# A small GpSimd fill behind each neighbour gather of a graph kernel's first two layers

## What is computed

```python
# layers 0 and 1, "untyped"
xn = layernorm(h); q, k, v = xn @ wq, xn @ wk, xn @ wv
scores = einsum('ehd,ehd->eh', q[dst], k[src]) * scale      # edges, and one self edge per node
attn = softmax of scores over the edges of each dst
agg = segment_sum(attn * v[src], dst)
h = h + agg @ wo + bo
h = h + gelu(layernorm(h) @ w1 + b1) @ w2 + b2
# layer 2, "typed"
mod_k = K[src] + 0.2 * rel_w[edge_type]
scores = einsum('ehd,ehd->eh', Q[dst], mod_k) / D ** 0.5
msgs = segment_sum(softmax(scores) * V[src], dst)            # V itself where a node has no edge
x = x + layernorm(msgs @ Wo + bo + node_features) * gamma + beta
```

## Time and profile before

| | |
|---|---|
| time before, median of 3 runs | 6028.8 us (6025.58 to 6051.66) |
| the profiled execution | 6041.55 us, of which the span is 6039.4 us |
| busy share of the span: DVE, PE, POOL, ACT | 58%, 54%, 46%, 31% |
| gathers of neighbours' rows (L1283) | 2430, mean 997 ns each |
| share of the 16 DMA engines, all queues | q0 (from POOL) 40.3%, q1 (from SP) 9.4% |
| moved | 886.73 MB, 147 GB/s over the span |
| granted TensorE clock, mean | 0.742 |

### The profile page before, as it was taken

The page is one execution under the profiler, slowest core; times in us unless marked ns, Lnnn a source line. Parts: engine busy times, 40 slices in busy tenths (PEclk is TensorE's granted clock), DMA queues, the critical chain, the costliest instruction groups (busy, mean ns, idle before and its releaser), DMA issues. The chain is left out here.

```text
span 6039.4 us, 88354 instructions
## 1 busy us (share of the span) xinstructions
PE 3256.9 (54%) x17373; PEld 2423.7 (40%) x17374; DVE 3499.7 (58%) x5216; ACT 1879.4 (31%) x4257; POOL 2782.5 (46%) x2783
## 2 busy tenths in 40 slices
PE   8575455455555555635545454455565545555655
PEld 6232334333333344523433343333344434444444
DVE  6441445545555555544555555555554758798887
ACT  3342232222222233323222222223334423334444
POOL 0330444544444444244454544444424557777664
PEclk9786677677777777867767777777787767666667
DMA  3343545545455444355554545544434546666654
GB/s 122 120 153 75 160 141 148 158 143 152 140 148 149 143 138 137 102 160 153 149 167 143 158 135 148 152 141 144 138 107 137 162 136 181 183 185 186 176 175 127
DMA packets 369280, 886.73 MB, mean 147 GB/s; under 512 B 140773, under 2 KB 153279, under 8 KB 369225
## 3 DMA queue, kind: packets, MB, share of 16 engines
q0 software_dynamic: 217200, 702.54, 40.3%
q1 hardware_dynamic: 151708, 182.79, 9.4%
q10 hardware_dynamic: 320, 0.84, 0.0%
HBM read 742.87 MB, written 143.30 MB: 147 GB/s over the span
## 5 line engine op out<-in xcount | busy, mean ns | idle before, releaser
L1283 POOL DMA_INDIRECT kv<-kv_dram,idx x2430 | 2421.5, 997 | 1121.8 <-issue 722.1
L2085 PE MATMUL ps_w<-w_ffn,shared 128*128 128x256 f32 x1568 | 567.9, 539 | 1423.8 <-ACT shared L1816 1326.9
L2085 PEld LDWEIGHTS ps_w<-w_ffn,shared 128*128 128x128 f32 x1568 | 432.0, 283 | 1559.5 <-ACT shared L1816 1367.3
L1411 DVE TENSOR_REDUCE sc<-products 128x32 f32<-128x1024 f32 (+2 forms) x654 | 784.3, 1211 | 17.2 <-DVE products L1404 11.8
L1991 PE MATMUL ps_acc<-ident,kv 128*128 128x128 f32 x4944 | 701.9, 305 | 49.0 <-issue 40.0
L1519 DVE TENSOR_TENSOR kv<-kv,ps_q 128x1024 f32<-128x1024 f32 x594 | 683.9, 1215 | 4.5 <-issue 0.3
L1991 PEld LDWEIGHTS ps_acc<-ident,kv 128*128 128x128 f32 x4944 | 645.1, 159 | 96.9 <-issue 69.6
L1816 ACT ACTIVATE shared<-ps_big,b 128x128 f32<-128x128 f32 x784 | 214.6, 380 | 1462.2 <-remote 1444.9
L1404 DVE TENSOR_TENSOR products<-kv,ps_q 128x1024 f32<-128x1024 f32 x436 | 523.4, 1219 | 52.1 <-issue 42.4
L1251 POOL DMA_INDIRECT kv_dram<-rec_out,scatter_to x98 | 100.3, 1024 | 849.3 <-issue 849.3
L2072 PE MATMUL ps_big<-xnaT,w_ffn 128*128 128x128 f32 x3136 | 393.4, 280 | 106.0 <-issue 102.1
(11 more groups left out here) (243 smaller groups left out, 5367.7 us busy)
## 6 DMA issues: line engine op xcount, KB each, us to landing
rec_dram<-rec_out SPq DMA_DIRECT2D x98, 512.0 KB
rec_in<-rec_dram SPq DMA_DIRECT2D x98, 512.0 KB
kv<-kv_dram,idx POOLq DMA_INDIRECT x2430
rec_by_node<-rec_in SPq DMA_DIRECT2D x49, 512.0 KB
windows<-kv SPq DMA_DIRECT2D x49, 384.0 KB
kv_dram<-rec_in SPq DMA_DIRECT2D x49, 256.0 KB
rec_out<-in_x SPq DMA_DIRECT2D x48, 128.0 KB
w_ffn<-in_L_gnn_w SPq DMA_DIRECT2D x4, 1024.0 KB
```

The source lines that it names most:

```text
L1283: pool.indirect_dma_start(kv[:, u * W + slot, :], None, kv_dram[l], bass.IndirectOffsetOnAxis(ap=idx[:, u, slot:slot + 1], axis=0)).then_i ...
L1411: nc.vector.tensor_reduce(scw[:, slice(c * CH * H, (c + 1) * CH * H) if isinstance(c, int) else bass.ds(c * (CH * H), CH * H)].rearrange(" ...
L2085: mm = nc.tensor.matmul(to, gT[:, f, :], w_2[:, f, :], start=False, stop=(f == KF - 1))
```

## The change

In layers 0 and 1 (`if not typed`) POOL runs, after each gather of a slot, a wait for the previous fill, a `settle` and a memset of a new tile `pause` of 128 partitions by 128 float32, which nothing reads. A new semaphore `pause` counts the memsets; one is added at the layer's start so that the first wait passes. So before the fill behind gather i may be issued, the fill behind gather i-1 has to be complete. The typed layer keeps its program but for one register move and one semaphore increment ahead of its loop.

```diff
+        pause = sb("pause", [P, 128])
...
-            "used", "taken", "query", "node", "zinit")}
+            "used", "taken", "query", "node", "zinit", "pause")}
...
                     scattered = Passed(pool, s["scat"], 16)
+                    paused = Passed(pool, s["pause"])
+                    pool.sem_inc(s["pause"], 1)
...
                                     bass.IndirectOffsetOnAxis(ap=idx[:, u, slot:slot + 1], axis=0)).then_inc(
                                         kv_sem[c], 16 if slot < c * CH + slots - 1 else 16 * (CH - slots + 1))
+                                if not typed:
+                                    paused.wait()
+                                    settle(pool)
+                                    nc.gpsimd.memset(pause[:], 0.0).then_inc(s["pause"], 1)
```

## The result

Against 6034.4 us for the kernel before (median of 4 runs, 6025.6 to 6051.7) the changed kernel takes **5760.8 us** (4 runs, 5748.6 to 5783.8): a ratio of 0.9551, 95% interval 0.9527 to 0.9574. The profiled execution took 5748.6 us with a span of 5746.6 at a mean granted clock of 0.743. The forecast was 5444 us.

What follows compares the result with a forecast made beforehand. No engine was full; closely following gathers on POOL stalled the others. 810 x 1.50 / 49 + 8.1 = 32.9 us a block, 1612 a layer, saved 585 us from 6041.55: 5457, median 5444 us; 8-in-10 range 5180 to 5990.

Steps and rivals of the forecast that it cites:

- the rest of the block: Untyped block's time beyond its gather steps: 18.0 us before, 8.1 us forecast if the stall goes.
- The step: Start to start of gathers in a burst: 1.25 us before, 1.50 forecast with the fill, bounds 1.37 and 1.78.
- the stall: In untyped blocks other engines hardly advance during a gather burst; gelu waits 714.4 us in layer 0; forecast to go.
- lost lead: POOL's sequencer can be only one gather ahead; priced at 3.6 us a block, inside the rest of the block.
- The mechanism: Other engines hardly advance while gathers follow at 1.25 us; at the typed layer's mean 1.39 most blocks run free.
- The wait: POOL's wait for the previous fill: costed at nothing within a burst, covered by the running gather's 0.95 us.
- Rival 1: Stall goes only by half: rest 13.05 us, block 37.9, about 5930 us; chance 0.22, shared with a step up to 1.78.
- Rival 2: Stall stays until the end of a longer burst, each fill paid in full: 6434 or 6888 us; chance 0.19.
- Rival 3: Relief and longer bursts cancel: some 6030 us, rest of the block near 14.1 us; chance 0.05.
- Gelu under 200 us a layer: Sign in ACT's waits: the gelu's 714 us per layer falls under 200.
- The gelu within the burst: Sign in one block's timeline: the gelu starts within the gather burst, no longer only at its end.
- Node gather about 4 us behind the last gather: Sign in one block's timeline on POOL: the node gather comes about 4 us after the block's last gather.

Runs made afterwards that it cites:

- e2: The changed kernel with a fill of one element instead of 128 columns, wait behind every gather kept; 0.960 of before on kind one, 1.217 on kind two.
- e5: The changed kernel with four counting sequencer instructions per gather in place of wait and fill; 0.980 of before on kind one, 1.147 on kind two.
- e1: The changed kernel with a 96-byte fill behind each gather but only one wait per chunk; 0.986 of before on kind one, 1.080 on kind two.
- e6: The changed kernel with wait, settle and fill only in the first three chunks of a block; 0.938 of before on kind one, 1.099 on kind two.
- e7: e1 with its fills and wait only in the first three chunks of a block; 0.987 of before on kind one.

## Why the prediction was wrong, step by step

**The mis-sized term is "the rest of the block".** The sum was 810 x 1.50 / 49 + 8.1 us. Measured, in layers 0 and 1 on kind one: steps 810 x 1.34 / 49 = 22.2 us and a rest of 1809 / 49 - 22.2 = 14.8 and 1722 / 49 - 22.2 = 13.0. The step was 0.16 us too long in my sum, worth 1620 x 0.16 = 259 us too much; the rest was too short by 6.7 and 4.9 us, 49 x 11.6 = 568 us too little. Their difference, 309 us, less the 15 that the typed layer won, is 294; the profiled execution (5748.6) stands 292 above the forecast for it (5457).

**What fills the rest.** The same kernel on kind two, without any crawl, has rests of 1747 / 49 - 22.2 = 13.5 and 1664 / 49 - 22.2 = 11.8 us. So of the 568 us, 49 x (5.4 + 3.7) = 446 are GpSimd's own and would be there without a crawl, and some 120 are the crawl that is left. What the stall still costs above GpSimd's own floor is 62 and 58 us a layer; but that floor is 1747 and 1664 us, not 1612. The stall itself is not gone: gelu and copy wait 725 us in layer 0, before 1054, on kind two 254. It is in large part covered by GpSimd's own time. The prediction priced the lost lead in that term at 3.6 us a block (3.2 by e2 less e5, up to 7.1 by e1) and gave the length of the program no price at all (2.5 us a block by e1, up to 6.5 by e5).

The missing price was a wrong reading of the change, not of the profile: four instructions per gather were counted as executed 810 times a layer, not as standing some 80 times in a loop's body. The prediction even cited the rule: the Trainium skill, Runtime: NRT & Kernel Launch, "Instruction fetch mechanics", says that a taken branch to a target outside the fetched window must wait for a DMA. I used it as a rival cause of the old stall and did not ask what it makes of a longer body. The trace agrees with it in kind: 37 packets before, 589 after, 5 in a gap of 9.14 us and none in one of 0.30 (both on kind two).

**The mechanism.** "The others start again when gathers stand further apart" is refuted at the steps that were tried on kind one with unbroken bursts (1.30 and 1.31 us: gains of 1.3 and 1.4%). The typed layer was not the experiment that I took it for: its mean step of 1.39 us includes gathers of 1.73 us beside quiet stretches, and it has the crawl as well (1448 us on kind one, 1292 on kind two, the same instructions). Whether a step of 1.5 us or more in unbroken bursts ends the crawl was not tried on kind one.

**The step.** 1.34 us, under my lower bound of 1.37. The fill is 0.22 us, as the iota row had it; wrong was that the pause of 0.30 would stand in full behind it. It shrank to 0.16.

**The wait** was costed at nothing within a burst. On kind two that is nearly right (the steps stay 1.34 us). On kind one it is what does the work (e2 against e1, e6 against e7), by breaks in the bursts or otherwise.

**Rival 1** (5700 to 5990, rest of the block 13.05) gives the time and the rest that were measured. That is luck in good part: it has half of the stall staying on the path. Of the 800 us that gelu and copy waited in layer 0 above their waits on kind two, 471 did stay, but GpSimd's own longer time lies over them and sets the block. **Rival 2** is refuted by the time: the kernel got faster, where it had 6434 us or more. Its sign came in part, as said next. **Rival 3** isn't what happened.

**The signs.** Fill 0.15 to 0.25 us: right (0.22). Gelu under 200 us a layer: right in the letter, but the wait moved to the copy. The gelu within the burst: wrong in two thirds of the blocks. In the rows above it starts at 1549.63, behind the last gather's start, because the copy ahead of it came only at 1547.95. In layer 0 it starts within a burst for 16 of 49 blocks, before for 3, on kind two for 45. Node gather about 4 us behind the last gather: 7.3 in the rows above. Typed layer unchanged: 1448 for 1463. Granted clock above 0.75: 0.75 and 0.76 in the untyped layers, 0.743 in the whole, so hardly.

## What to carry to other kernels

Ask of every instruction added to a loop written out how many times it *stands* in the program, beside how often it runs, and look at the row of instruction packets before and after: here 37 became 589, and on kind two each block paid for it behind its last gather. When a stall is relieved, forecast the floor of the engine that caused it with its new instructions, not with those it had. And a relief of something that not every chip shows has to be measured on several: this change is worth 4.5% on one kind and costs 24% on the other. Where kind one is what counts, e6 (0.938) is better than the change; on kind two the kernel before is the fastest of all.

## What the hardware showed that was not expected

- Two kinds of chip run the same program at 6036 and at 4340 us, a factor of 1.39. What differs in the traces is how sequencers fare beside indirect DMAs on GpSimd (a pair of SP's issues 3.85 and 5.60 us, or 1.22), not the engines' own work: DVE is busy for 1022 and 1018 us in layer 0 of the changed kernel, POOL for 1047 and 1044. Why the chips differ stays open.
- A small fill behind an indirect DMA adds less than its own length (the fill of 0.22 us adds 0.09 to the step): 0.22 us for 128x128, 0.117 for one element (the mean in layer 0 of e2), 0.195 for 96 bytes, all of them mostly within the 0.30 us between two indirect DMAs. With 384 columns the step is 1.55 us.
- On a chip that crawls, what takes GpSimd's lead away can pay, be it a wait behind each gather (e2, 4.0%) or, less, counting instructions (e5, 2.0%). Whether the fetching of its own program can is open (layer 0 of e6 takes 1703 us against 1780 of layer 1, but e1 and e7 take the same time). That e6 fetches in layer 0 and not in layer 1, with as many instructions in each, was not explained.
